# Five small reorderings at the seam between two sequences of a scan-and-experts kernel

## The reference, cut to what matters

```python
x = x + attn(layernorm(x))
x = x + ffn(layernorm(x))
# attn(h): h = rmsnorm(h) * w_norm_in
z, x, B, C, dt_raw = split(h @ w_in_proj)            # 256, 256, 512, 512, 8 columns
x  = silu(causal_conv(x, 4 taps));  dt = softplus(dt_raw @ w_dt + b_dt)
y  = chunked_scan(x, mean_per_head(dt), B, C) + x * D
y  = rmsnorm(y * silu(z)) * w_norm_out;  out = h + y @ w_out_proj
# ffn(f): 2 shared experts (mean) + the best 2 of 4 routed experts, weighted,
# each relu(f @ w1 + b1) @ w2 + b2 with 512 hidden columns
```

## Time and profile before

| | us |
|---|---|
| median of 3 runs | 567.92 |
| range of the runs | 567.83 to 567.97 |
| the profiled execution's own time | 568.1 |
| its span, first to last instruction | 566.3 |
| TensorE matmul busy | 535.4 (95%) |
| VectorE busy | 448.0 (79%) |
| ScalarE busy | 356.7 (63%) |
| GpSimd busy | 173.4 (31%) |
| mean granted TensorE clock | 0.996 |

### The profile page before, as it was taken

The page is one execution under the profiler, slowest core; times in us unless marked ns, Lnnn a source line. Parts: engine busy times, 40 slices in busy tenths (PEclk is TensorE's granted clock), DMA queues, the critical chain, the costliest instruction groups (busy, mean ns, idle before and its releaser), DMA issues.

```text
span 566.3 us, 11586 instructions
## 1 busy us (share of the span) xinstructions
PE 535.4 (95%) x3851; PEld 420.4 (74%) x3851; DVE 448.0 (79%) x1053; ACT 356.7 (63%) x768; POOL 173.4 (31%) x235
## 2 busy tenths in 40 slices
PE   7887989999999899999999999999999999999996
PEld 5666767868787777877787677877787687877774
DVE  5889877978689787888878787897878888775654
ACT  4794688647676477736786386755886477652442
POOL 3064115630153203630145202622036211432010
PEclk9999999999999999999999999999999999999998
DMA  6550025100560007300381005600162004700120
GB/s 198 169 156 30 0 90 162 59 1 1 150 177 2 2 5 219 105 1 0 101 194 30 0 0 170 154 0 0 41 207 76 1 0 140 170 1 1 35 64 19
DMA packets 37433, 41.46 MB, mean 73 GB/s; under 512 B 3522, under 2 KB 27796, under 8 KB 37396
## 3 DMA queue, kind: packets, MB, share of 16 engines
q1 hardware_dynamic: 36820, 40.85, 25.7%
q10 hardware_dynamic: 576, 0.14, 0.1%
HBM read 37.83 MB, written 3.15 MB: 72 GB/s over the span
## 4 chain that ended last, share of the span: by engine, by line
PE 46%; DVE 30%; issue 9%; ACT 7%; POOL 3%; DMA 3%; DVEq 1%; ACTq 0%; SPq 0%; POOLq 0%
PE bank L432 6%; DVE act_l L1316 6%; PE bank L554 5%; PE bank L433 5%; PE bank L434 5%; DVE cv L1160 4%; PE bank L666 4%; PE bank L667 4%; PE bank L668 4%; PE bank L564 3%; DVE mg L1194 2%; DVE late L1324 2%; PE bank L587 2%; ACT act_h L903 2%; DVE dsum L1176 2%
## 5 line engine op out<-in xcount | busy, mean ns | idle before, releaser
L1316 DVE SCALAR_TENSOR_TENSOR act_l<-bank,act_h 128x512 fp32r<-128x512 f32 x192 | 131.5, 687 | 50.4 <-ACT act_h L903 47.5
L903 ACT ACTIVATE act_h<-bank 128x512 fp32r<-128x512 f32 x192 | 114.5, 596 | 89.1 <-PE bank L434 85.5
L432 PE MATMUL bank<-fTl,w1h 128*128 128x512 f32 x192 | 86.5, 450 | 8.2 <-DVE act_l L1316 7.4
L1565 POOL TENSOR_TENSOR late<-late 128x512 f32<-128x512 f32 x31 | 39.8, 1284 | 163.9 <-DVE late L1324 163.9
L923 ACT ACTIVATE seg<-seg,lneg 128x128 f32<-128x128 f32 x256 | 81.2, 393 | 2.7 <-DMA seg<-lc_rows 2.7
L666 PE MATMUL bank<-act_l,w2h 128*128 128x512 f32 x192 | 77.8, 405 | 3.2 <-DVE act_l L1316 2.6
L667 PE MATMUL bank<-act_h,w2l 128*128 128x512 f32 x192 | 76.1, 396 | 0.0
L434 PE MATMUL bank<-fTh,w1h 128*128 128x512 f32 x192 | 75.7, 394 | 0.0
L668 PE MATMUL bank<-act_h,w2h 128*128 128x512 f32 x192 | 75.6, 394 | 0.0
L433 PE MATMUL bank<-fTh,w1l 128*128 128x512 f32 x192 | 75.6, 394 | 0.0
L1552 POOL TENSOR_TENSOR xw<-xs,seg 128x128 f32<-128x128 f32 x48 | 20.2, 422 | 130.2 <-ACT seg L923 91.6
(11 more groups left out here) (179 smaller groups left out, 1041.9 us busy)
## 6 DMA issues: line engine op xcount, KB each, us to landing
seg<-lc_rows SPq DMA_DIRECT2D x32, 512.0 KB, 3.7
late<-gk_rows SPq DMA_DIRECT2D x8, 1024.0 KB, 8.9
grow<-lc_rows SPq DMA_DIRECT2D x48, 128.0 KB, 4.9
x_in<-L_attn_hidden_dram SPq DMA_DIRECT2D x8, 256.0 KB, 3.1
out_dram<-late SPq DMA_DIRECT2D x8, 256.0 KB, 5.3
late<-L_ffn_sw_dram SPq DMA_DIRECT2D x2, 512.0 KB, 6.2
late<-L_ffn_rw_dram SPq DMA_DIRECT2D x1, 1024.0 KB, 6.5
CT<-L_attn_w_in_proj_dram SPq DMA_DIRECT2D x1, 512.0 KB, 5.4
```

Source lines behind the costliest of these rows:

```text
L432: mm(dst, stat_h, mov_l, start=True, stop=False)
L903: nc.scalar.activation(act_h[:, b % RING, :], HID[b % 2][:], ACT.Relu).then_inc(act_h_ready, 1)
L1316: v_.scalar_tensor_tensor(act_l[:, r, :], HID[b % 2][:], 0.0, f(act_h[:, r, :]), ALU.max, ALU.subtract)\
```

## The change

It does five things. GpSimd's `rsqrt_y` goes ahead of `add_term(prev, 2)`. `sum_squares` goes behind the output products of chunk 0 alone (four records) and no longer behind those of chunks 0 and 1. The gating of chunk 3 goes, for all sequences but the first, out of `attend` to a place behind `act_low` of block 19. In the opening dt's weights are split ahead of dt's sums on ScalarE and VectorE. And the first sequence's dt sums go to HID[0], so that their first product waits for the high part of h alone; for the other sequences the bank and the first wait stay, and the same wait stands once more ahead of the second product.

```diff
--- before.py
+++ after.py
@@ -314,6 +314,9 @@
 
             return MAIN[3] if is_seq(s, n_seq - 1) and (b < 8 or b // 4 in (3, 5)) else FOUT
 
+        def z_bank(s):
+            return HID[0] if is_seq(s, 0) else TR
+
         def block_at(i, prev, older):
 
             q, b = (older, NBLK - LATE + i) if i < LATE else (prev, i - LATE)
@@ -501,9 +504,13 @@
             def dt_sums(s):
                 if is_seq(s, 0):
                     pe.wait_ge(wz_set, 3)
+                    pe.wait_ge(hTh_ready, 1)
+                else:
+                    pe.wait_ge(hTl_ready, nth(s, 1, 1))
+                sums = z_bank(s)
+                mm(sums[:], wz_all[:], hTh[:], start=True, stop=False)
                 pe.wait_ge(hTl_ready, nth(s, 1, 1))
-                mm(TR[:], wz_all[:], hTh[:], start=True, stop=False)
-                mm(TR[:], wz_high[:], hTl[:], start=False, stop=True).then_inc(z_psum, 1)
+                mm(sums[:], wz_high[:], hTl[:], start=False, stop=True).then_inc(z_psum, 1)
 
             def x_tokens(s, i):
                 pe.wait_ge(b_ready, nth(s, 3, i + 1))
@@ -773,7 +780,7 @@
                 square_rows(s)
                 for c in range(NCH):
                     out_projection(s, c)
-                    if c == 1:
+                    if c == 0:
                         sum_squares(s)
                 if not is_seq(s, n_seq - 1):
                     proj(s + 1, 1)
@@ -844,7 +851,7 @@
 
             def z_copy(s):
                 act.wait_ge(z_psum, nth(s, 1, 1))
-                nc.scalar.copy(zT[:], TR[:]).then_inc(z_high_ready, 1)
+                nc.scalar.copy(zT[:], z_bank(s)[:]).then_inc(z_high_ready, 1)
 
             def x_copy(s, b):
                 act.wait_ge(proj_psum, made(s, b))
@@ -1035,9 +1042,9 @@
                 hT(0)
                 act.wait_ge(wbc_w_in, 16)
                 w_high(B0, 512, 512)
-                z_copy(0)
                 act.wait_ge(wdt_in, 6 * 16)
                 nc.scalar.copy(wdt[:], wdt_raw[:]).then_inc(wdt_set, 1)
+                z_copy(0)
                 act.wait_ge(cols_psum, 1)
                 nc.scalar.mul(cols[:, 0:24], MAIN[3][:, 0:24], 1.0 / P).then_inc(cols_set, 1)
                 nc.scalar.copy(cols[:, 24:34], MAIN[3][:, 24:34]).then_inc(cols_set, 1)
@@ -1146,7 +1153,7 @@
 
             def z_low(s):
                 dve.wait_ge(z_high_ready, nth(s, 1, 1))
-                v_.tensor_tensor(zT[32:48, :], TR[32:48, :], f(zT[32:48, :]), ALU.subtract).then_inc(z_ready, 1)
+                v_.tensor_tensor(zT[32:48, :], z_bank(s)[32:48, :], f(zT[32:48, :]), ALU.subtract).then_inc(z_ready, 1)
 
             def conv(s, b, taps):
                 for k in taps:
@@ -1208,8 +1215,8 @@
                     for b in range(NB):
                         v_.scalar_tensor_tensor(yT[:, b, at(c)], yT[:, b, at(c)], d_col[:, b:b + 1], MAIN[0][:, at(b)],
                                                 ALU.mult, ALU.add).then_inc(y_steps, 1)
-                    dve.wait_ge(y_steps, nth(s, 8, 2 * c + 2))
-                    v_.tensor_tensor(yT[:, :, at(c)], yT[:, :, at(c)], szT[:, :, at(c)], ALU.mult).then_inc(yz_ready, 1)
+                    if c < NCH - 1 or is_seq(s, 0):
+                        gated(s, c)
 
             def next_state(s, c):
                 first = (0, 2, 5)[c]
@@ -1228,6 +1235,10 @@
                     else:
                         v_.tensor_tensor(state[q, c % 2, :, d], own[q, :, d], state_m[q, :, d], ALU.add).then_inc(state_step, 1)
                 dve.wait_ge(state_step, nth(s, 8, first + 2))
+
+            def gated(s, c):
+                dve.wait_ge(y_steps, nth(s, 8, 2 * c + 2))
+                v_.tensor_tensor(yT[:, :, at(c)], yT[:, :, at(c)], szT[:, :, at(c)], ALU.mult).then_inc(yz_ready, 1)
 
             def mean_square(s):
                 dve.wait_ge(ssq_psum, nth(s, 1, 1))
@@ -1385,6 +1396,8 @@
                         z_low(s + 1)
                     if (new := block_at(i, prev, older)) and not (i == 0 and prev is not None):
                         act_low(*new)
+                    if s is not None and i == NBLK - 1:
+                        gated(s, NCH - 1)
                     if older is not None and i == (7 if s is not None or prev is None else 9):
                         store(older)
                     if s is not None and i in (15, 18):
@@ -1436,9 +1449,9 @@
                 w_low(Z0, 0, DI, 2)
                 hT_low(0)
                 w_low(B0, 512, 512, 3)
-                z_low(0)
                 dve.wait_ge(wdt_set, 1)
                 v_.tensor_tensor(wdt[64:80, :], wdt_raw[64:80, :], f(wdt[64:80, :]), ALU.subtract).then_inc(wdt_set, 1)
+                z_low(0)
                 w_low(C0, 1024, 512, 4)
                 dve.wait_ge(bdt_in, 16)
                 dt_add(0, 0)
@@ -1586,10 +1599,10 @@
                         rsqrt1(s + 1)
                     if prev is not None and i in (16 + LAG, 19 + LAG):
                         add_term(prev, (i - 15 - LAG) // 4)
+                if s is not None:
+                    rsqrt_y(s)
                 if prev is not None and s is not None:
                     add_term(prev, 2)
-                if s is not None:
-                    rsqrt_y(s)
 
             bodies(pool, opening, body)
 
```

## The result

The changed kernel took 560.21 us (median of 4 runs, 559.42 to 560.94), the kernel before beside it 567.88 us (median of 4, 566.93 to 567.97). The ratio is 0.9868, with a 95% interval of 0.985 to 0.9887: 7.7 us less. The profiled execution took 559.76 us with a span of 558.0, 8.3 us less than the span of before.

A forecast was written before the change was run, and what follows sets the result against it. It took VectorE's residual sums, waiting for GpSimd's power step at the seams, as the bound. Six seams x 1.05 + 0.45 opening - 0.1 = 6.65 us less gave 561.3 us on the median's scale, range 559.8 to 564.2.

The forecast's parts named there:

- two inputs of the residual sums that meet: At a seam between bodies: GpSimd's power step and the last output product both arrive near 318.60 us, releasing VectorE's residual sums.
- Low part ahead of the gating: At the seam, block 19's low part starts 0.37 us earlier on VectorE, and all TensorE work behind it moves by 0.37.
- thin cover: At the seam, ScalarE's square of chunk 3 is done only 0.05 us before TensorE's sums of squares begin.
- Sum of squares behind four records: At the seam, VectorE's mean square starts at 317.29 us instead of 318.01, with no idle time in front.
- Power step ahead of the addition: At the seam, GpSimd's power step starts at 317.53 us instead of 318.59; the expert's addition behind it costs nothing.
- What is late next: At the seam, residual sums need power step and last output product; they start at 318.75 instead of 319.80, gaining 1.05 us.
- The opening: Start of the kernel: earlier dt product and weights' split gain 0.45 us, bounds 0.2 and 0.65.
- The last seam: After sequence 7: TensorE goes through fill products, gain 0; 0.1 us of loss for first and last seam together.
- Output products late: Rival at the seams: last output product binds the residual sums, 0.68 us a seam, 563.5 us; chance 0.12.
- Most given back: Rival at the seams: another input holds later steps, only TensorE's 0.37 us stays, 565.4 us; chance 0.06.
- Held residual sums: Rival at the seams: GpSimd's addition holds VectorE's residual sums until it ends, slower, 568.5 us; chance 0.05.
- a rule: VectorE instructions with two SBUF inputs and GpSimd instructions reading SBUF exclude each other; costed at nothing for the residual sums.

## Why the prediction was right

It gave 561.3 us, faster, with a range of 559.8 to 564.2. The step that carried it, two inputs of the residual sums that meet, held. Point by point:

*Low part ahead of the gating.* Predicted 0.37 us for TensorE, measured 0.40 and 0.38 a step later. The thin cover held: the fourth square ends at 310.91, the sums start at 311.08. The weight load of the sums does name the square as its releaser, where it named none before, so this input may have no slack left; that was not tested.

*Sum of squares behind four records.* Predicted 0.72 us for the mean square, measured 0.82. Alone it gave nothing and taken back it cost 0.3 us a period, as the order of the inputs says.

*Power step ahead of the addition.* Predicted 1.06, measured 1.16 us. The addition's readers had room.

*What is late next.* The last output product, by its releaser in the list of waits. Predicted gain 1.05 us a seam, measured from the gap between skip sums and residual sums: 1.14, 1.15, 1.08, 1.08, 1.08 and 1.08, together 6.6 where the sum had 6.3. In the period of the loop 1.05 of it arrives, which is the number of the sum.

*The opening* was mis-sized: 0.45 us taken, 0.77 measured at the first dt addition (13.83 to 13.06), of which 0.08 came with an earlier normalisation of the input. ScalarE's C part moved by 0.68: z's copy started 0.38 earlier (11.27 to 10.89), and 0.30 came from the weights' copy, which no longer stands between the two. So the term should have been at its upper bound, 0.65. By the time of the whole it is not resolved; at the first seam, with profiles of like clock side by side, it is 0.8 to 0.9 us.

*The last seam* was put at a loss. The residual sums started 0.34 us earlier than the rest had moved (513.86 to 505.71, against 507.47 to 499.66 for the skip sums), and TensorE took 0.24 of it. That the fill products hide all of it was wrong. TensorE's lead over the kernel before grew from 7.78 to 8.02 us at block 22, in front of which block 20's low part had ended at 516.61 in the kernel before, 0.06 us ahead of L432 (516.67), and ends at 508.46 now, 0.29 us ahead of it (L435, 508.75).

Beyond these, the profiled difference of 8.3 us holds some luck. In the third body ScalarE waited for the decay rows 1.70 us before and 1.20 after, since the write of the rows ahead of them landed sooner (SyncE waited 3.0 us for it before, 1.6 after), which no part of the change touches. That body shrank by 1.58 us (65.91 to 64.33) where the loop's shrank by 1.05, so some 0.5 us is luck. At the very end the last transposes took less: the step from the last expert output to the final sum grew the lead from 7.95 to 8.31 us. There TensorE had gone idle, and the granted clock over the last 6 us was 0.65 in the profile of before (1.15 us busy) and 0.82 after, so part of these 6 us was at the lower level of 1.2 GHz, a smaller part after; the four last transposes took 0.98 and 0.63 us. Neither of the two profiles had the stretch at the lower clock ahead of the first seam. The medians differ by 7.7 us, 1.0 more than the 6.65 of the sum. The interval of the ratio reaches from 6.4 to 8.5 us, so that this 1.0 is not resolved; the profiles have places for it, some 0.3 us at the opening and 0.3 at the last seam with the 0.1 us of loss that did not come, and luck as above for the rest.

*The rivals.* Output products late: no, though they are now the latest input. Most given back: no. Held residual sums: no, 1.13 us beside the addition. The Trainium skill (SBUF — State Buffer, section Who interferes with whom), from which the prediction weighed a rule, also says that VectorE modes which use two port pairs, and `tensor_scalar` can enter one, are blocked for a whole instruction by a GpSimd instruction that was issued first. The normalisation beside the addition agrees, with one instruction of 1310 ns in place of 345; in which mode it ran no trace shows.

## What to carry to other kernels

When several inputs release one step, undo each alone and add each alone: the part that only works with the others shows 0 when added and its full share when removed, and neither number is its worth. Look at what a moved instruction will lie beside on its new stretch: an addition on GpSimd was free beside sums that read PSUM and cost 1 us beside a normalisation from SBUF to SBUF. And read a small gain from the period of a loop in the profile, where it stands at 0.1 us, when the whole shifts by a microsecond from run to run. Before such a shift is put down to loads, compare the granted clock of the two profiles window by window: here 3.4 us at the lower clock made 1.5 us, nearly twice what the opening's reordering gained, and profiles sorted by it showed the gain that the medians hid.

## What the runs showed that was not expected

The same addition, 1.29 us long, cost VectorE nothing beside four instructions with a PSUM input and 0.96 us (2.08 against 1.12) beside four that read and write SBUF alone and have one tensor input.

The granted clock fell for 3.4 us just ahead of the first seam in seven of thirteen profiles, with either opening, and put that seam 1.5 us later. The profiles of the eight kernels with the new opening so have it at 51.8 to 52.3 us or at 53.3 to 53.4, and none in between.
